# Layer norms of two blocks moved into the last units of the first attention, with roots by Newton steps

## What is computed

```python
y = x + (attn @ Wo.T + bo)
return (y - mu) / jnp.sqrt(var + EPS) * gamma + beta
...
x = x + _L0_attn_a_ref(_layernorm(x, axis=-1), ...)
x = x + _L0_ffn_ref(_layernorm(x, axis=-1), ...)
```

## Time and profile before

| | |
|---|---|
| median of 3 runs | 2078.3 us (2077.17 to 2080.09) |
| profiled execution | 2082.57 us, of which the span is 2080.7 |
| busy in the span | PE 1965.4 (94%), DVE 1507.5 (72%), ACT 1481.2 (71%), POOL 1279.6 (61%) |
| chain that ended last | PE 86%, DVE 8%, POOL 2%, issue 2%, ACT 1% |

### The profile page before, as it was taken

How to read it: one execution, slowest core, us unless ns; L and a number is a source line. 1 busy time by engine, 2 the same in 40 slices (tenths; PEclk the granted TensorE clock), 3 DMA queues, 4 the chain that set the end, 5 groups by cost and what they waited for, 6 DMA issues and landing times.

```text
span 2080.7 us, 51602 instructions
## 1 busy us (share of the span) xinstructions
PE 1965.4 (94%) x21751; PEld 1435.1 (69%) x21751; DVE 1507.5 (72%) x2818; ACT 1481.2 (71%) x1812; POOL 1279.6 (61%) x687
## 2 busy tenths in 40 slices
PE   4999999999999999999999967899999999999997
PEld 3466666666666666666666544678888787888885
DVE  7888888788888888888888756566676666667642
ACT  2798998998989988999989852355545455554563
POOL 4899999998999999999999852131312223131200
PEclk8999999999999999999999988899999999999999
DMA  5100110110011001101100010000000000000000
GB/s 137 32 20 15 32 32 10 25 32 21 18 28 32 17 17 33 25 17 25 32 17 17 2 52 1 0 1 1 1 1 1 1 1 1 1 1 1 1 1 21
DMA packets 45013, 37.67 MB, mean 18 GB/s; under 512 B 8304, under 2 KB 44144, under 8 KB 44528
## 3 DMA queue, kind: packets, MB, share of 16 engines
q1 hardware_dynamic: 43824, 33.60, 6.6%
q10 hardware_dynamic: 960, 0.79, 0.2%
HBM read 8.15 MB, written 1.05 MB: 4 GB/s over the span
## 4 chain that ended last, share of the span: by engine, by line
PE 86%; DVE 8%; POOL 2%; issue 2%; ACT 1%; ACTq 0%; DMA 0%; POOLq 0%; DVEq 0%
PE ST L1354 10%; PE ST L1355 10%; PE OO L1491 8%; PE RING L1229 7%; PE OO L1298 6%; PE OO L1300 6%; PE OO L1297 6%; PE OO L1229 3%; PE RING L1444 3%; PE ST L1514 3%; PE ST L1491 3%; PE ST L1518 3%; PE RING L1424 3%; PE ST L1516 3%; POOL PAB L517 2%
## 5 line engine op out<-in xcount | busy, mean ns | idle before, releaser
L517 POOL TENSOR_TENSOR PAB<-PR,PAB 128x1024 f16<-128x1024 f32 x342 | 723.7, 2131 | 62.3 <-ACT PAB L655 62.3
L655 ACT ACTIVATE PAB<-ST,exp_scale 128x1024 f16<-128x1024 f32 x512 | 567.0, 1107 | 0.0
L903 DVE TENSOR_REDUCE maxes<-RING 128x1 f32<-128x512 f32 x679 | 450.9, 685 | 132.8 <-PE RING L1229 131.5
L1297 PE MATMUL OO<-VP,PAB 128*128 128x66 f16 x4096 | 446.9, 193 | 2.4 <-POOL PAB L517 2.4
L1298 PE MATMUL OO<-VP,PAB 128*128 128x64 f16 x4096 | 447.5, 194 | 0.0
L1300 PE MATMUL OO<-VP,PAB 128*128 128x66 f16 x4096 | 445.5, 192 | 0.0
L653 ACT ACTIVATE PR<-ST,exp_scale 128x1024 f32<-128x1024 f32 x342 | 381.2, 1115 | 85.7 <-PE ST L1355 83.1
L1297 PEld LDWEIGHTS OO<-VP,PAB 128*128 128x128 f16 x4096 | 380.5, 96 | 78.0 <-issue 15.8
L1298 PEld LDWEIGHTS OO<-VP,PAB 128*128 128x128 f16 x4096 | 377.3, 97 | 61.3
L1354 PE MATMUL ST<-QL,KH 128*128 128x512 f16 x1024 | 388.8, 380 | 2.1 <-ACT PAB L655 1.2
L1355 PE MATMUL ST<-QH,KL 128*128 128x512 f16 x1024 | 389.0, 380 | 0.0
(11 more groups left out here) (202 smaller groups left out, 3260.0 us busy)
## 6 DMA issues: line engine op xcount, KB each, us to landing
KH<-HS SPq DMA_DIRECT2D x120, 64.0 KB, 2.0
QL<-HS SPq DMA_DIRECT2D x64, 64.0 KB, 2.0
QL<-LS SPq DMA_DIRECT2D x64, 64.0 KB, 2.0
QH<-HS SPq DMA_DIRECT2D x64, 64.0 KB, 2.0
KL<-LS SPq DMA_DIRECT2D x60, 64.0 KB, 2.0
X<-in_L_attn_a_x SPq DMA_DIRECT2D x4, 256.0 KB, 3.9
SHARED<-in_rope_cos SPq DMA_DIRECT2D x1, 1024.0 KB, 4.9
SHARED<-in_rope_sin SPq DMA_DIRECT2D x1, 1024.0 KB, 7.9
```

The source lines that it names most:

```text
L517: pool.tensor_tensor(PB[:, s, :], PRA[g % PR_SLOTS], PA[:, s, :], ALU.subtract).then_inc(p_low_ready, 1)
L655: act.activation(PA[:, step % SLOTS_A, :], ST[step % 2][:, :], ACT.Exp, scale=scale).then_inc(sa.exps, 1)
L903: dve.reduce_max(maxes[:, i // BLOCKS, i % BLOCKS:i % BLOCKS + 1], bank[:, :], X_AXIS).then_inc(sa.ring_taken, 1)
L1297: pe.matmul(o, high, v[:, 0:V2_AT], start=(m == 0 and qt == 0), stop=False, skip_group_check=True)
```

## The change

Four of the eight norms, y and x of blocks 0 and 1, are made inside the loop of 512 steps. On DVE, in steps 62.6 to 63.5, one piece stands at the end of each step: statistics of y0, its norm, statistics of y1, its norm, x0 (addition and statistics), its norm, x1, its norm. `normalise_here` makes these norms without ACT: an addition of eps, two integer instructions for a first guess of the reciprocal root and three Newton steps of three instructions, twelve instructions of 128x4, each waiting for the one before; then the four of 128x128. POOL multiplies y0 with gamma behind the subtraction of 62.7 and y1 behind that of 63.2. PE waits for the taking of y2 before its last three steps of products, and puts the transposes of x0 and x1 and the pieces of block 0's hidden layer among them and among the last transposes and output; hidden layers 0 and 1 and output 0 come ahead of block 2. ACT makes four roots instead of eight there.

```diff
-SETTLE = [("y", 0), ("y", 1), ("y", 2), ("x", 0), ("x", 1), ("y", 3), ("x", 2), ("x", 3)]
+SETTLE = [("y", 0), ("y", 1), ("x", 0), ("x", 1), ("y", 2), ("x", 2), ("y", 3), ("x", 3)]
+SETTLED_EARLY = 4
...
@@ POOL @@
+            def apply_gamma(b):
+                pool.wait_ge(y_applied, b + 1)
+                y = XN[:, b * BT:(b + 1) * BT, :]
+                pool.tensor_tensor(y, y, gamma_b[:, :].unsqueeze(1).broadcast_to((P, BT, D)), ALU.mult
+                                   ).then_inc(y_ready, 1)
...
                 p_low(step, g)
+                if (u, step) == (ITER_A * UNITS_A - 2, 7):
+                    apply_gamma(0)
+                if (u, step) == (ITER_A * UNITS_A - 1, 2):
+                    apply_gamma(1)
+            for b in range(2, BLOCKS):
+                apply_gamma(b)
...
@@ ACT @@
-            for i in range(5):
-                deviations(BLOCKS + i)
-            transposed_block(BLOCKS, O[0][:, :])
...
+            act.wait_ge(fw_in, 48)
+            transposed_block(BLOCKS, spare_a)
+            deviations(BLOCKS + 4)
+            transposed_block(BLOCKS + 1, spare_a)
+            relus(0, 0)
+            deviations(BLOCKS + 5)
+            deviations(BLOCKS + 6)
+            relus(0, 1)
+            transposed_block(BLOCKS + 2, O[0][:, :])
+            relus(0, 2)
             deviations(BLOCKS + 7)
...
@@ DVE @@
+            def normalise_here(n, b, src, signal):
+                slot = n % SLOTS_LN
+                var, root, half = meanvar[:, slot, :, 1], rstd[:, slot, :], std[:, slot, :]
+                dve.wait_ge(var_ready, n + 1)
+                link(dve.tensor_scalar(half, var, EPS, None, ALU.add))
+                link(dve.tensor_scalar(step_ln[:, :].bitcast(I32), half.bitcast(I32), 1, None, ALU.arith_shift_right))
+                link(dve.tensor_scalar(root.bitcast(I32), step_ln[:, :].bitcast(I32), -1.0, float(0x5F3759DF), ALU.mult,
+                                       ALU.add))
+                for turn in range(3):
+                    link(dve.scalar_tensor_tensor(step_ln[:, :], root, -0.5, root, ALU.mult, ALU.mult))
+                    link(dve.tensor_tensor(step_ln[:, :], step_ln[:, :], half, ALU.mult))
+                    ins = dve.scalar_tensor_tensor(root, step_ln[:, :], 1.5, root, ALU.add, ALU.mult)
+                    if turn < 2:
+                        link(ins)
+                ins.then_inc(rstd_ready, 1)
+                dve.wait_ge(rstd_ready, n + 1)
+                for i in range(BT):
+                    ins = dve.tensor_scalar(XN[:, b * BT + i, :], src[:, b * BT + i, :], meanvar[:, slot, i, 0:1],
+                                            rstd[:, slot, i:i + 1], ALU.subtract, ALU.mult)
+                ins.then_inc(signal, 1)
...
+                place = g - (ITER_A * G_A - STEPS_A - 2)
+                if 0 <= place < 2 * SETTLED_EARLY:
+                    (normalise_settled if place % 2 else settle)(place // 2)
...
-            settle(0, 1, 2)
-            for i in range(3):
-                normalise_settled(i)
...
+            settle(4)
+            normalise_settled(4)
+            normalise_a(UNITS_A - 1, ITER_A * UNITS_A)
+            take_turned(sa, RING3[(END_A - 2) % 3], END_A - 2)
+            settle(5)
+            take_output(sa, RING3[(END_A - 1) % 3], END_A - 1, XN, BLOCKS - 1)
+            settle(6)
+            normalise_settled(5)
+            normalise_settled(6)
+            take_ffn(0, 0)
+            settle(7)
+            normalise_settled(7)
...
@@ PE @@
-            for g in range(ITER_A * G_A - LAG_A, ITER_A * G_A):
-                for j in range(2):
-                    pv_a(g, j)
-            turned_a(END_A - 2, BLOCKS - 1, ITER_A * UNITS_A)
-            output_a(END_A - 1, END_A - 2, ITER_A - 1)
-            pe.wait_ge(sa.ring_taken, END_A)
...
-            turn_x(4)
-            turn_x(5)
-            hidden(0, 0)
-            turn_x(6)
-            hidden(0, 1)
-            ffn_out(0, 0)
-            turn_x(7)
-            hidden(0, 2)
+            pe.wait_ge(sa.ring_taken, END_A - 2)
+            for k in range(LAG_A):
+                for j in range(2):
+                    pv_a(ITER_A * G_A - LAG_A + k, j)
+                if k < 2:
+                    turn_x(4 + k, spare_a)
+            hidden_part(0, 0, 0)
+            turned_a(END_A - 2, BLOCKS - 1, ITER_A * UNITS_A)
+            hidden_part(0, 0, 1)
+            output_a(END_A - 1, END_A - 2, ITER_A - 1)
+            hidden_part(0, 0, 2)
+            hidden_part(0, 0, 3)
+            hidden(0, 1)
+            pe.wait_ge(sa.ring_taken, END_A)
+            ffn_out(0, 0)
+            turn_x(6)
+            hidden(0, 2)
             ffn_out(0, 1)
+            turn_x(7)
             hidden(0, 3)
```

## The result

The changed kernel takes 2084.7 us in the median of 18 runs (2079.7 to 2087.5), the kernel before 2078.3 in 18: ratio 1.0031, 95% interval 1.0024 to 1.0038. It is slower by 6.4 us. The profiled execution took 2084.66 with a span of 2082.8.

The account below looks back on a forecast made before the run. POOL bounds the attention's end, then DVE's norms for 28 us, then PE. Behind the products 16 us are saved, but these end 22 later: net +6.4 on the median 2078.3 gives 2084.7, range 2072 to 2090.

Parts of the forecast that it names:

- the mark: End of the last first-layer product of feed-forward 0 (L1387) on PE: 1262.2 before, forecast 1268.5.
- First norm: Norm of y0 on DVE from step 62.7: two links wait for subtractions, ten run free; ends at 1205.5.
- Second norm: Norm of y1 on DVE: three links wait for the subtractions of 63.0 to 63.2, nine run free; ends at 1216.1.
- the rule that the prediction weighed: A DVE instruction with two SBUF inputs contends with a GpSimd one reading SBUF; the later blocks fully, so all links wait.
- The division: normalise_a of unit 62 on DVE in step 63.3, for which PE waits: ends at 1218.7 instead of 1204.98.
- The clock: PE's restart after some 13 us idle: 2.9 us at half clock, the rest at full; 4.1 us, to 1222.8.
- Norm of x1: On DVE beside POOL's last three subtractions: three links wait, by 1233.4, nine and the tensor_scalars end by 1236.4.
- Tail: From the end of the attention's products to the last first-layer product of feed-forward 0: 26 us instead of 42, 16 saved.
- Free links: Rival: POOL's blocking doesn't touch the small DVE links, which take 0.2 us amid subtractions; 2070.4 us, faster; chance 0.14.
- Only float tensor_scalars wait: Rival: on DVE the first link and the final four wait, integer and two-input links don't; 2078.7 us, no change; chance 0.18.
- A slower clock: Rival: PE's half clock lasts 6 us instead of 2.9 at both restarts, 1.5 each; 2087.7 us; chance 0.12.
- its rule of one wait per POOL instruction: A DVE instruction waits for the end of the POOL instruction it meets: 2.09 us a link instead of 0.205.

Follow-up runs that it names:

- the links alone: Kernel before, nothing moved, plus twelve dependent 128x4 Newton instructions on DVE behind the taking of y1, on values that nothing uses: 2088.6 us, ratio 1.0048.
- the norms in PSUM: Changed kernel with an operand of each Newton link in a PSUM bank and the four 128x128 as scalar_tensor_tensor reading the root there: 2071.9 us, ratio 0.9964.

## Why the prediction was right

The time came out as forecast, and the steps with it. That it did so to the tenth is luck: the sum's own steps give 6.3, the mark moved by 5.7, and the medians differ by 6.4. In the times of before (after plus 2.80):

- **First norm.** Two links wait, ten run free at POOL's gamma: forecast end 1205.5, measured 1205.5.
- **Second norm.** Three links wait; the end at 1215.8 was forecast as 1216.1. In detail it differs: the first link found POOL at its gamma's end and took 0.17, and the fourth waited instead. L818 is a two-input instruction, of which no row of before told; its 2.04 agrees with the rule that the prediction weighed (the Trainium skill, "SBUF — State Buffer", Who interferes with whom).
- **The division** ended at 1218.2 (forecast 1218.7), the last subtraction at 1233.1 (1233.4), the taking of y2 at 1236.5 (1237.1), the mark at 1267.9 (1268.5).
- **The clock.** Half clock behind the first idle stretch lasted 4.5 us, not 2.9. From the division to ACT's first exponential it made 4.3 us against 4.1 forecast: products, transposes and scores took 3.9 us at half clock, so 1.9 at full, where I had 2.7, and the two errors cancelled, which is luck as well.
- **Norm of x1.** Four links wait (0.72, then three of 2.04 to 2.06) where I had three, since the norm starts earlier; it ends at 1235.9 (1236.4).
- **Tail.** From the products to the mark 41.9 us before, 26.5 after: 15.4 saved where I had 16, and the products ended 21.1 later where I had 22: here, too, the errors offset each other.

The rivals fell at known places. Free links: the 2.01 to 2.06 above, and the links alone, 9.7 us. Its price was near, though: it had 2070.4, and the norms in PSUM, which do run free in the places of the change, gave 2071.9. Only float tensor_scalars wait: integer and two-input links wait as long. A slower clock: 4.5 us at half behind the first stop and 3.3 behind the second, where that rival needed 6 each.

The prediction bounded the wait by what POOL still has to run. That held in a kernel where it wasn't fitted: with the links alone, six waits until POOL ran out at 1211.4. One row of before doesn't fit its rule of one wait per POOL instruction: the L908 of 5.31 us, at 1154.98, passes two ends of subtractions (1156.10 and 1158.19) and ends with the third (1160.26). No link in any run did so, and no run shows why. What the prediction didn't look for is a way around the price: with the operands in another memory, and the four 128x128 instructions in a two-input form for it, the same norms in the same places make the kernel faster by 0.36%.

## To carry to other kernels

In this kernel a chain of small dependent VectorE instructions beside a GpSimd that never pauses cost one GpSimd instruction per link (2.05 us, not 0.2), in each form tried: tensor_scalar, tensor_tensor and scalar_tensor_tensor. Idle time of VectorE in such a stretch isn't free time. With one operand of each link in a free PSUM bank the chain ran beside GpSimd at 0.15 to 0.17 us a link. Then let GpSimd find its inputs ready, and look at what TensorE waits for behind the moved work: behind both waits of the change its granted clock stood at 0.50.

## What the runs showed of the hardware

The wait goes both ways: beside subtractions X += XN took 0.95 to 2.51 us instead of 0.68, and the subtraction issued behind it 2.57 to 2.59 instead of 2.12 (the runs with the norms in PSUM). One PSUM operand is enough to escape, for integer and float, one input and two: 0.15 to 0.17 us a link in every one of them. Not every instruction in SBUF waits: beside running subtractions a tensor_reduce from 128x16 to 128x4 took 0.17 us (L907 at 1195.21 before), and the first four statistics instructions of y0 took 0.85 together (1194.33 after). TensorE's clock came back later without any change of the work: some 35 us ahead of the change's first instruction, behind the same stall of PE (4.4 us), the granted clock was 0.58 and then 1.00 in two stretches of 4 us before, 0.50 and 0.74 in the two of after that answer to them, and the trace of after loses 1.35 us there. That is why the comparison starts at the taking of y0.
